# The last image's stores and the order of set-up work at the two ends of the heads stage of a vision tower

## The reference, cut to what matters

```python
h = h + _L0_ffn_ref(_layernorm(h, axis=-1), ...)
h = h + _L1_attn_ref(_layernorm(h, axis=-1), ...)
# in _L1_attn_ref:
q = _heads(x @ Wq)
kv = _heads(x @ Wkv)
q = _rope(q)
kv = _rope(kv)
q = q * DH ** (-0.5)
lkv = _ln(kv, ln_g, ln_b)
attn_lat = jax.nn.softmax(jnp.einsum('bid,bkd->bik', q_lat, kv), axis=-1)
attn_ctx = jax.nn.softmax(jnp.einsum('bid,bkd->bik', q_ctx, kv_ctx), axis=-1)
```

## Time and profile before

| what | us |
|---|---|
| median of 3 runs | 4409.71 |
| lowest and highest | 4407.69 and 4420.83 |
| the profiled execution's own time | 4417.4 |
| its span in the trace | 4415.7 |

### The profile page before, as it was taken

How to read it: one execution, slowest core, us unless ns; L and a number is a source line. 1 busy time by engine, 2 the same in 40 slices (tenths; PEclk the granted TensorE clock), 3 DMA queues, 4 the chain that set the end, 5 groups by cost and what they waited for, 6 DMA issues and landing times. The chain is left out here.

```text
span 4415.7 us, 74709 instructions
## 1 busy us (share of the span) xinstructions
PE 3907.1 (88%) x23896; PEld 2372.0 (54%) x23898; DVE 2477.4 (56%) x4583; ACT 1494.8 (34%) x2982; POOL 1333.3 (30%) x1520
## 2 busy tenths in 40 slices
PE   8899778799999997665999999999995989899996
PEld 8788445466666665331333333333333765577774
DVE  1576468422222222886877778777853547644443
ACT  0222124211111111342677777777771221111110
POOL 0222013244444443564001000001102121177774
PEclk9999999899999998775899999999996879999998
DMA  6221111332232221345333322233305431277776
GB/s 222 64 63 53 32 40 44 97 63 62 62 62 62 62 62 29 110 142 116 47 50 53 56 45 45 45 46 56 55 9 137 122 97 42 77 174 174 173 173 152
DMA packets 336020, 361.74 MB, mean 82 GB/s; under 512 B 50460, under 2 KB 297203, under 8 KB 334191
## 3 DMA queue, kind: packets, MB, share of 16 engines
q1 hardware_dynamic: 252255, 274.75, 25.4%
q0 software_dynamic: 61312, 63.66, 9.4%
q10 hardware_dynamic: 22288, 20.93, 1.5%
HBM read 247.51 MB, written 117.00 MB: 83 GB/s over the span
## 5 line engine op out<-in xcount | busy, mean ns | idle before, releaser
L2096 DVE TENSOR_REDUCE at_mx<-psum 128x1 f32<-128x998 f32 (+1 forms) x768 | 885.1, 1190 | 257.7 <-PE psum L1921 257.2
L2051 ACT ACTIVATE at_p<-psum 128x512 f32<-128x512 f32 (+3 forms) x1536 | 851.8, 588 | 303.4 <-PE psum L1995 273.6
L1995 PE MATMUL psum<-at_q,at_k 99*128 99x512 bf16 (+3 forms) x1536 | 522.4, 383 | 22.0 <-issue 16.9
L1921 PE MATMUL psum<-at_k,at_q 96*128 96x512 bf16 (+3 forms) x1536 | 476.0, 393 | 70.5 <-POOL at_identb L1878 32.9
L1981 PE MATMUL psum<-at_p,at_v 128*32 128x486 f32 (+3 forms) x3072 | 408.4, 604 | 1.0 <-ACT at_p L2051 0.7
L1893 POOL DMA_DIRECT2D o_rows<-at_o x96 | 48.7, 507 | 1150.0 <-DVE at_mx L2096 833.0
L1256 ACT ACTIVATE ex_silu<-psum 128x384 f32<-128x384 f32 (+1 forms) x288 | 131.8, 457 | 767.4 <-PE psum L1200 637.6
L1995 PEld LDWEIGHTS psum<-at_q,at_k 99*128 99x128 bf16 (+1 forms) x1536 | 155.7, 102 | 429.1 <-ACT at_p L2051 272.0
L1287 DVE TENSOR_TENSOR ex_hT<-ex_silu,psum 128x384 f32<-128x384 f32 (+1 forms) x288 | 147.6, 513 | 415.2 <-ACT ex_silu L1256 270.3
L1222 PE MATMUL psum<-ex_wd,ex_hT 128*128 128x192 f32 (+1 forms) x1728 | 291.5, 327 | 0.0
L1921 PEld LDWEIGHTS psum<-at_k,at_q 96*128 96x128 bf16 (+1 forms) x1536 | 151.8, 105 | 234.1 <-DVE at_mx L2096 64.0
(11 more groups left out here) (386 smaller groups left out, 7128.2 us busy)
## 6 DMA issues: line engine op xcount, KB each, us to landing
mx_wd<-in_e_dT SPq DMA_DIRECT2D x72, 288.0 KB, 4.0
qk_parts<-hd_parts SPq DMA_DIRECT2D x32, 579.4 KB, 3.7
at_k<-qk_parts SPq DMA_DIRECT2D x144, 128.8 KB, 5.3
at_q<-qk_parts SPq DMA_DIRECT2D x144, 124.8 KB, 4.7
tok_p<-in_x SPq DMA_DIRECT2D x12, 1176.0 KB, 22.7
mx_wg<-in_e_gT SPq DMA_DIRECT2D x72, 192.0 KB, 2.5
mx_wu<-in_e_uT SPq DMA_DIRECT2D x72, 192.0 KB, 2.9
v_rows<-hd_v_out SPq DMA_DIRECT2D x8, 1536.0 KB
```

The source lines that it names most:

```text
L1921: mm = pe.matmul(psum[0:ctx_rows[t], 3 + 2 * ((PRO + n) % 2) + k, 0:w], Q[v][0:R6, j * 1024 + 128 * t:j * 1024 + 128 * t + ctx_rows[t]], K ...
L1995: pe.matmul(psum[0:n, i % RING, 0:w], K[u][:, j, 128 * t:128 * t + n], Q[u][:, j * 1024 + at:j * 1024 + at + w], start=True, stop=True).th ...
L2051: act.activation(P[0:n, c % 2, j, 0:w], psum[0:n, i % RING, 0:w], ACT.Exp).then_inc(exp_ready, 1)
L2096: dve.tensor_reduce(mx[0:ctx_rows[t], j * CT + t:j * CT + t + 1], pair(n)[0:ctx_rows[t], 0:CTX], AX_X, ALU.max).then_inc(s_free, 1)
```

## The change

Three edits. (1) The buffers `hd_parts` and `hd_v_out`, the semaphores of their stores and a new one, `first_ones`, are made by `heads_leaving` in the scope around experts, heads and attend. SP no longer waits for the stores at the end of heads; it does so at the start of attend, ahead of `load(0, 1)`. That scope has a clear and a barrier of its own, so there is one pair more after attend. (2) The ones of K buffer 0 are written in heads, behind POOL's other memsets; in attend POOL first sets `mx` and the three counters, then `identb` and `sums`, and then the ones of K buffers 1 and 2; PE waits for `identb` only ahead of `turn_maxima` and for the ones ahead of `quad(0)`; DVE waits for `mx` alone. (3) In heads the memset of `rows` comes first, on a semaphore of its own, and SP's first load waits for that one alone.

```diff
@@ -1389,7 +1389,14 @@
-def phase_heads(nc, psum, inp, y, qk_parts, v_rows, ident, ident_in, consts, consts_in, first, loaded, v_loaded):
+def heads_leaving(ctx, nc):
+
+    sb, sem = names(ctx, nc)
+    return (sb("hd_parts", [DP, 3, 2 * D // DP, SEQ], BF16), sb("hd_v_out", [128, (KT + 1) * HEADS, HV]),
+            [sem(f"hd_parts_out{q}") for q in range(2 * D // DP)], sem("hd_v_stored"), sem("at_first_ones"))
+
+
+def phase_heads(nc, psum, inp, y, qk_parts, v_rows, ident, ident_in, consts, consts_in, first, loaded, v_loaded, leaving):
@@ -1410,7 +1417,7 @@
         rot = sb("hd_rot", [128, 2, KT + 1, NQ])
-        parts = sb("hd_parts", [DP, 3, QC, SEQ], BF16)
+        parts, v_out, parts_out, v_stored, first_ones = leaving
         left = sb("hd_left", [DP, RING, 512])
@@ -1419,14 +1426,13 @@
         vrstd = sb("hd_vrstd", [128, NH])
-        v_out = sb("hd_v_out", [128, NH, HV])
         stats = sb("hd_stats", [128, KT + 1, 6])
...
-        set_up = sem("hd_set_up")
+        set_up, rows_set = sem("hd_set_up"), sem("hd_rows_set")
         rows_in = sem("hd_rows_in")
@@ -1440,9 +1446,8 @@
         v_ready = sem("hd_v_ready")
-        parts_out, v_stored = [sem(f"hd_parts_out{q}") for q in range(QC)], sem("hd_v_stored")
         NT = KT + 1
-        SETUP = 7
+        SETUP = 6
@@ -1463,7 +1468,7 @@
-            sp.wait_ge(set_up, SETUP)
+            sp.wait_ge(rows_set, 1)
             load(0)
@@ -1495,21 +1500,20 @@
             store(B - 1)
-            for q in range(QC):
-                sp.wait_ge(parts_out[q], 16 * B)
-            sp.wait_ge(v_stored, 32 * B)
...
         def _(pool):
+            pool.memset(rows[:, KT, :], 0.0).then_inc(rows_set, 1)
             pool.memset(eps[:], EPS).then_inc(set_up, 1)
             pool.memset(v_out[:, :, DH:HV], 1.0).then_inc(set_up, 1)
-            pool.memset(rows[:, KT, :], 0.0).then_inc(set_up, 1)
...
             pool.wait_ge(set_up, SETUP)
+            pool.memset(first[1][R6:RM, :, :], 1.0).then_inc(first_ones, 1)
+            pool.wait_ge(first_ones, 1)
@@ -1744,7 +1748,8 @@
-def phase_attend(nc, psum, inp, qk_parts, v_rows, o_rows, recips, ident, ident_in, first, loaded0, v_loaded0, project, project_in):
+def phase_attend(nc, psum, inp, qk_parts, v_rows, o_rows, recips, ident, ident_in, first, loaded0, v_loaded0,
+                 leaving, project, project_in):
@@ -1780,7 +1785,8 @@
-        identb_ready, ones_set = sem("at_identb_ready"), sem("at_ones_set")
+        _, _, parts_out, v_stored, first_ones = leaving
+        identb_ready, mx_set, sums_set, ones_set = (sem(f"at_{n}") for n in ("identb_ready", "mx_set", "sums_set", "ones_set"))
         loaded = [loaded0] + [sem(f"at_loaded{u}") for u in (1, 2)]
@@ -1844,6 +1850,10 @@
+
+            for stored in parts_out:
+                sp.wait_ge(stored, 16 * B)
+            sp.wait_ge(v_stored, 32 * B)
             load(0, 1)
@@ -1864,18 +1874,17 @@
         def _(pool):
-            for u in range(3):
-                pool.memset(K[u][R6:RM, :, :], 1.0).then_inc(ones_set, 1)
-            pool.wait_ge(ones_set, 3)
-            pool.memset(mx[:], 0.0).then_inc(ones_set, 1)
-            pool.wait_ge(ones_set, 4)
-            pool.memset(sums[:], 1.0).then_inc(ones_set, 1)
-            pool.wait_ge(ones_set, 5)
+            pool.memset(mx[:], 0.0).then_inc(mx_set, 1)
             pool.memset(none[:, 0:1], 0.0).then_inc(s_free, S_FREE0)
...
             pool.tensor_copy(identb[:], ident[:]).then_inc(identb_ready, 1)
+            pool.memset(sums[:], 1.0).then_inc(sums_set, 1)
+            pool.wait_ge(sums_set, 1)
+            for u in (1, 2):
+                pool.memset(K[u][R6:RM, :, :], 1.0).then_inc(ones_set, 1)
+                pool.wait_ge(ones_set, u)
@@ -1911,9 +1920,6 @@
         def _(pe):
-            pe.wait_ge(identb_ready, 1)
-            pe.wait_ge(ones_set, 5)
-
             def by_query(v, t, j, base, n):
@@ -2016,11 +2022,14 @@
             by_latent(0, -1, CT * QH + 1)
+            pe.wait_ge(identb_ready, 1)
             turn_maxima(MSTEP, -1, CT * QH + 3)
...
+            pe.wait_ge(first_ones, 1)
+            pe.wait_ge(ones_set, 2)
             quad(0, 0, 0, PRO, 2, None)
@@ -2070,7 +2079,7 @@
         def _(dve):
-            dve.wait_ge(ones_set, 5)
+            dve.wait_ge(mx_set, 1)
@@ -3418,13 +3427,14 @@
         with ExitStack() as quads:
-            first = quad_buffers(quads, nc, 0)
+            first, leaving = quad_buffers(quads, nc, 0), heads_leaving(quads, nc)
             with ExitStack() as middle:
...
                 phase_experts(nc, psum, inp, xg, y, ids, ident, ident_in, heads, heads_in)
-                phase_heads(nc, psum, inp, y, qk_parts, v_rows, ident, ident_in, heads, heads_in, first, loaded, v_loaded)
+                phase_heads(nc, psum, inp, y, qk_parts, v_rows, ident, ident_in, heads, heads_in, first, loaded, v_loaded,
+                            leaving)
             phase_attend(nc, psum, inp, qk_parts, v_rows, o_rows, recips, ident, ident_in, first, loaded, v_loaded,
-                         project, project_in)
+                         leaving, project, project_in)
         slots = sb("slot_rows", [128, NSL], I32)[:]
...
         with ExitStack() as late:
```

## The result

Five runs of the changed kernel had a median of 4395.51 us (4385.18 to 4401.51), five of the kernel before, beside them, one of 4414.44 (4407.69 to 4420.83; the three runs of the first table are among these five). The ratio is 0.9955, with an interval of 0.9938 to 0.9973: 19.9 us less, between 12 and 27. About half of these 9.5 us is the kernel before itself, whose median over five runs was 4.7 above that of the first three. The other half is a gain of 19.9 instead of 23.7, and the experiments ask whether these 4 us are missing from the change or only from this measurement.

What follows compares the result with a forecast made beforehand. SP's waits for stores, then POOL's memsets, were taken to bound the heads-attend border, and memsets, load, DVE the start of heads; 2.5 + 10.5 + 11.2 - 0.5 = 23.7 us off 4409.7 gave 4386.0, range 4377 to 4399.

Steps and rivals of the forecast that it cites:

- What bounds the stretch: Border between heads and attend: SP, waiting for its stores, is last at the barrier; POOL's memsets come next; PE, DVE, ACT idle 23 us.
- The stores, 10.5: End of heads: SP no longer waits for its stores before the barrier, 10.5 us gained, bounds 0 and 10.6.
- Rival 1: Border of heads: SP's drain before the barrier waits for the stores after all, the 10.5 come back, 4396.5 us; chance 0.05.
- Rival 2: Heads and attend: memsets block DVE, 7.0 us beside the reductions and 3.5 in heads lost, 4396.5 us; chance 0.04.
- The order, 11.2: Start of attend: PE's first matmul comes 0.3 us behind POOL's first instruction instead of 11.49, 11.2 us gained, upper bound 11.4.
- The first load, 2.5: Start of heads: the load waits for one memset, 2.5 us gained if what follows keeps its length, bounds 0 and 2.5.
- rival 3: Heads gives its head start back, something tied to a time outside the stage setting the pace; 2.5 us vanish, 4388.5; chance 0.05.
- The memsets beside DVE, 0: Start of attend: 7.0 us of POOL memsets beside DVE's reductions cost 0; the other bound is a full block, 7.0.
- the bound of 3.5: Where a DVE tensor_scalar met one of the new memsets, the gain would be smaller by up to that memset's 3.5 us.
- The cover of 14 us: Attend: loads of quad 1, moved behind SP's store waits, land near 2064, PE wants them at 2078.3 at the earliest; cost 0.
- The second clear, 0.5: Behind attend: one more clear and barrier on the path, 0.5 us lost, bounds 0.1 and 1.0.
- Rival 4: Attend: TensorE's low clock lasts on into the quads, 16 us a quad; with three quads 4434 us; chance 0.02.

## Why the prediction was right

- **What bounds the stretch.** SP last at the barrier, POOL's memsets next: both held, each shown by an edit that moved it alone. The first is shown a second way by the values' stores, which moved the barrier when they were taken from SP.
- **The stores, 10.5.** The trace has 10.6; alone, timed and with the second clear, 5.8 (2 to 9.7), where the two terms make 10.0. The time alone does not confirm the size. Rival 1, the barrier that waits for stores, is out: SP's drain took 0.2 us while both groups of stores were in flight. The trace was needed for that: rivals 1 and 2 were priced at 4396.5, and the measured 4395.5 lies nearer to them than to the forecast.
- **The order, 11.2.** The trace has 11.2; alone, timed, 14.2 (9 to 19.5).
- **The first load, 2.5.** The trace has 2.2; its own time, 4.9 (0 to 10), is too coarse to size it. The sum said "if what follows keeps its length", and in the first profile it didn't, by 6.8. That looked like rival 3, at a greater price than that rival had. Eleven profiles and the start put off by 21 us show that it was not: the length goes with the clock. Why the clock falls differently from run to run stays open.
- **The memsets beside DVE, 0.** Right for the reductions, with four times the memsets. The prediction says that the trace of before has no reduction from PSUM beside POOL; it has, if only beside POOL's short DMA issues: from 2219.84 to 2224.4 nine of them ran beside L2096, two of whose reductions, begun at 2221.47, took 2.30, as elsewhere in the loop. For the tensor_scalars the bound of 3.5 was a real danger, avoided by the 4.2 us between them, which the prediction had put at about the same (1740.5 and 1744.6). Rival 2 is out for this change.
- **The cover of 14 us** was about 16.
- **The second clear, 0.5**, was 0.6.
- **Rival 4**, the low clock on into the quads, didn't occur. The prologue, from PE's first matmul to the first scores of quad 0, and the stretch from 2104 to 3254, in the same view as above:

```profile
2044.90:2094.54 49.64, 41.59 (x94) 6.57 (x94) 47.08 (x47) 0.00 (x0) 7.33 (x4) 0.50 0.59 108
2104.00:3254.00 1150.00, 1100.23 (x8597) 379.47 (x8595) 908.77 (x954) 857.77 (x1615) 100.72 (x197) 0.99 0.31 47
```

  The granted clock was 0.99 in the long stretch, where it had been 0.98. In steps of 1 us it rises to 1.00 at 2104.2, 9.6 us behind quad 0's first score matmul; before, it rose at 2122.6, 8.5 behind it (2114.1). The 49.6 us of the prologue stayed at 0.50 again, with PE busy for 41.6 of them.

The forecast in us, 4386.0, missed by 9.5: 4.7 from a median of three taken as the kernel's time, 3.8 from the size of the gain, of which the repeated measurements give back 2.8, and 1.0 by which the ratio (19.9) and the difference of the medians (18.9) differ. None of the four terms was mis-sized by more than 0.3 in the trace. What moved the forecast is the spread, which the prediction had put at some 5 for a median of three, and it did move by that. It is luck that the spread did not add 3.5 us more: the time would then have lain outside the range with every term right.

## What to carry to other kernels

At a border where all engines meet, list when each engine ends its stream and ask whether its last wait is for something that the next stage needs at once; here the wait for stores in flight was not. What goes first behind the border is what the first consumer waits for, and the rest goes beside its work, but not beside operations that the writer can block. To size a change of half a per cent, add up local distances between named rows of each trace; the ends of two traces gave 15.9 us here for terms that make 23.4.

## What the runs showed of the hardware

- A memset on POOL of 3x4120 bf16 (3.53 us) held up one tensor_scalar on DVE from 0.37 to 3.07 us, until the memset's end; reductions from PSUM stayed at 1.157 us each beside eight of them.
- With the same instructions, PE's busy time over one stretch of 293 to 300 us varied between 184.0 and 191.4 us with the granted clock (0.75 and 0.73), and the stage's length followed it nearly one to one, although DVE was busy for 231 us of it.
- A drain of SP with stores in flight took 0.2 us; SP's waits for them, begun right behind the barrier, ended 9 us later (6.0 and 3.2).
- A prologue of 49.6 us with PE busy for 41.6 of them ran at a granted clock of 0.50 throughout.
